# First image of an attention and expert-routing kernel: weights loaded by ScalarE's queue beside x in halves, v of image 1 between two maxima, the row of maxima ahead of k's remainder

## What is computed

```
q = jnp.einsum('mc,bcn->bmn', wq, xf)          # 32 x 1024 for each of 4 images
k = jnp.einsum('mc,bcn->bmn', wk, xf)
v = jnp.einsum('mc,bcn->bmn', wv, xf)
att = jnp.einsum('bmi,bmj->bij', k, q)
att = jax.nn.softmax(att, axis=2)
agg = jnp.einsum('bij,bmj->bmi', att, v)
out = x + jnp.einsum('cm,bmn->bcn', wo, agg).reshape(b, c, h, w)
...
t = t + _L1_attn_ref(_ln_t(t))                 # softmax(t t') t over 1024 tokens
t = t + _L1_ffn_ref(_ln_t(t), ...)             # router, best 2 of 8 experts
```

## Time and profile before

| what | us |
|---|---|
| median of 3 runs | 219.84 (218.81 to 220.49) |
| the profiled execution, its own time | 220.04 |
| its span in the profile | 218.3 |
| TensorE matmul busy in the span | 203.7 |
| VectorE busy | 144.7 |
| ScalarE busy | 107.5 |
| GpSimd busy | 62.1 |

### The profile page before, as it was taken

How to read it: one execution, slowest core, us unless ns; L and a number is a source line. 1 busy time by engine, 2 the same in 40 slices (tenths; PEclk the granted TensorE clock), 3 DMA queues, 4 the chain that set the end, 5 groups by cost and what they waited for, 6 DMA issues and landing times.

```text
span 218.3 us, 2929 instructions
## 1 busy us (share of the span) xinstructions
PE 203.7 (93%) x1073; PEld 104.7 (48%) x1073; DVE 144.7 (66%) x359; ACT 107.5 (49%) x166; POOL 62.1 (28%) x75
## 2 busy tenths in 40 slices
PE   6799998989999899998999999899999999898993
PEld 2463744454634335553443545344344433387773
DVE  2579947978564994566488754727693372898970
ACT  2540676548644646476275536656544666301110
POOL 8222021403000300003003359800359750027250
PEclk9799999999999999999999999999999999999999
DMA  4853000000000000000000000020000002000021
GB/s 107 148 128 67 3 0 0 0 2 3 2 0 0 0 0 3 0 0 0 3 2 0 0 3 2 0 48 0 3 0 0 0 3 50 0 0 3 0 48 48
DMA packets 3341, 3.67 MB, mean 17 GB/s; under 512 B 2176, under 2 KB 2432, under 8 KB 3328
## 3 DMA queue, kind: packets, MB, share of 16 engines
q1 hardware_dynamic: 3328, 3.50, 7.5%
HBM read 2.45 MB, written 1.05 MB: 16 GB/s over the span
## 4 chain that ended last, share of the span: by engine, by line
PE 66%; DVE 22%; ACT 4%; POOL 3%; DMA 2%; issue 2%; SPq 0%; DVEq 0%; POOLq 0%
PE acc L489 21%; DVE rowmax L1108 9%; PE ring L550 6%; PE ring L595 6%; PE ring L551 5%; PE ring L482 5%; PE ring L464 4%; PE acc L625 3%; POOL sm L367 3%; PE ring L442 2%; DMA xin<-in_x 2%; PE ring L526 2%; PE ring L537 2%; PE ring L443 2%; DVE stats L1141 1%
## 5 line engine op out<-in xcount | busy, mean ns | idle before, releaser
L900 ACT ACTIVATE prob<-ring,shift 128x1024 f32<-128x1024 f32 x32 | 35.6, 1112 | 27.6 <-PE ring L551 27.5
L1108 DVE TENSOR_REDUCE rowmax<-ring 128x1 f32<-128x1024 f32 x32 | 38.0, 1218 | 13.4 <-PE ring L464 13.3
L367 POOL TENSOR_TENSOR sm<-sm,minus_half 128x8 f32<-128x8 f32 x8 | 15.8, 1974 | 101.8 <-DVE sm L1151 101.8
L897 ACT ACTIVATE prob<-ring 128x1024 f32<-128x1024 f32 x32 | 31.9, 1023 | 17.8 <-PE ring L482 17.7
L489 PE MATMUL acc<-prob,u 128*64 128x512 f32 x128 | 31.0, 606 | 0.0
L489 PE MATMUL acc<-prob,val 128*64 128x512 f32 x128 | 31.0, 605 | 0.0
L1247 DVE TENSOR_TENSOR prod<-ring,gate 128x1024 f32<-128x1024 f32 x16 | 19.4, 1220 | 9.3 <-PE ring L595 8.8
L550 PE MATMUL ring<-zst 128*128 128x512 f16 x64 | 24.5, 384 | 0.4 <-DVE rowmax L1108 0.4
L551 PE MATMUL ring<-zsw,zst 128*128 128x512 f16 x64 | 24.3, 379 | 0.0
L464 PE MATMUL ring<-qst,kst 96*128 96x512 f32 x64 | 22.6, 437 | 0.5 <-DVE rowmax L1108 0.4
L482 PE MATMUL ring<-kst,qst 98*128 98x512 f32 x64 | 21.3, 425 | 0.8 <-DVE rowmax L1108 0.4
(11 more groups left out here) (156 smaller groups left out, 312.1 us busy)
## 6 DMA issues: line engine op xcount, KB each, us to landing
xin<-in_x SPq DMA_DIRECT2D x8, 256.0 KB, 4.1
out<-ob SPq DMA_DIRECT2D x6, 128.0 KB, 2.3
e_in<-in_L_ffn_expert_w SPq DMA_DIRECT2D x2, 128.0 KB
out<-ob SPq DMA_DIRECT2D x4, 64.0 KB, 2.0
eb_in<-in_L_ffn_expert_b SPq DMA_DIRECT2D x8, 2.0 KB
wo<-in_L_conv_wo SPq DMA_DIRECT2D x2, 8.0 KB, 2.5
r_in<-in_L_ffn_router_w SPq DMA_DIRECT2D x2, 2.0 KB
w<-in_L_conv_wq SPq DMA_DIRECT2D x1, 16.0 KB, 3.5
```

Of the source, the lines that this page charges most:

```text
L367: pool.tensor_tensor(sm[:, 3, :], sm[:, 2, :], minus_half[:, :], ALU.pow).then_inc(s_rs, 1)
L897: act.activation(prob1[:, j % DEEP, :], flat(filled(act, f"st{j}", b)), ACT.Exp).then_inc(s_p1, 1)
L900: act.activation(prob2[:, j % DEEP, :], flat(filled(act, f"s{j}", b)), ACT.Exp, bias=shift[:, :], accum_out=rsum2[b % 2][:, j:j + 1]).then ...
L1108: dve.tensor_reduce(rowmax[:, tile:tile + 1], flat(filled(dve, f"mx{tile}", b)), AX.X, ALU.max).then_inc(s_mx, 1)
```

## The change

Three things change, all in the first 27 us. **Loads:** the three weight transfers are issued by ScalarE's queue, ahead of everything else on ScalarE; SyncE's queue loads x of image 0 in four transfers of 64 x 512, and ScalarE rounds the first half as soon as it is there. `w1` is written by one instruction in place of three, the second half of x is rounded behind the weights, and q's first projection no longer waits for v's weights. **v of image 1** is projected by TensorE between the maxima of tiles 5 and 6 of image 0, in place of after k of image 1; three pairs of filler matmuls go. ScalarE copies it out ahead of q and k of image 1. **The row of maxima** of image 0 is copied by VectorE ahead of k's remainder of image 1.

```diff
--- before.py
+++ after.py
@@ -41,7 +41,8 @@
 
 
 
-HEAD = [("w3", 0), ("q", 0), ("k", 0), ("vx", 0)] + per_tile("mx", 0) + [("q", 1), ("k", 1), ("vx", 1), ("mr", 0)]
+HEAD = [("w3", 0), ("q", 0), ("k", 0), ("vx", 0)] + per_tile("mx", 0)[:6] + [("vx", 1)] + per_tile("mx", 0)[6:] + [
+    ("q", 1), ("k", 1), ("mr", 0)]
 
 FIRST = [("st0", 0), ("st1", 0), ("mx0", 1), ("st2", 0), ("mx1", 1), ("st3", 0), ("mx2", 1), ("mx3", 1), ("st4", 0),
          ("mx4", 1), ("st5", 0), ("mx5", 1), ("st6", 0), ("mx6", 1), ("st7", 0), ("mx7", 1), ("mr", 1), ("po", 0)]
@@ -189,6 +190,7 @@
         s_w3 = sem("w3_loaded")
         s_wol = sem("wo_loaded")
         s_ew = sem("experts_loaded")
+        s_x0 = [sem(f"x0_part_loaded{part}") for part in range(2)]
         s_x = [sem(f"x_loaded{b}") for b in range(B)]
         s_wr1 = sem("weights_rounded")
         s_wts = sem("weights_split")
@@ -298,9 +300,10 @@
                 for h in range(2):
                     sp.dma_start(xin[h * C:(h + 1) * C, b, :], x[b].rearrange("c h w -> c (h w)")).then_inc(s_x[b], 16)
 
-            load_x(0)
-            for n, w in enumerate((wq, wk, wv)):
-                sp.dma_start(w3[n * M:(n + 1) * M, :, :], w.unsqueeze(1).to_broadcast([M, 2, C])).then_inc(s_w3, 16)
+            first = x[0].rearrange("c h w -> c (h w)")
+            for part in range(2):
+                for h in range(2):
+                    sp.dma_start(xin[h * C:(h + 1) * C, 0, chunk(part)], first[:, chunk(part)]).then_inc(s_x0[part], 16)
             sp.wait_ge(s_const, 1)
             for h in range(2):
                 sp.dma_start(wo4[:, 2 * h, :], wo).then_inc(s_wol, 16)
@@ -447,6 +450,8 @@
 
             def project_v(b):
                 buf = take("vx", b)
+                if b:
+                    pe.wait_ge(s_xs, b + 2)
                 for tile in range(T):
                     toks = xst[b % 2][:, col(tile):col(tile) + P]
                     o = (tile % 4) * (M + C)
@@ -631,25 +636,28 @@
                     pe.matmul(bank[:, :], filler[:, 0:P], filler[:, :], start=True, stop=True)
 
             pe.wait_ge(s_filler, 1)
-            keep_clock(9)
+            keep_clock(8)
             buf = take("w3", 0)
             pe.wait_ge(s_const, 2)
             pe.wait_ge(s_w3, 3 * 16)
             pe.transpose(buf[:, 0, 0:ROW], w3[:, :, :].rearrange("p a c -> p (a c)"), ident[0:ROW, 0:ROW]).then_inc(s_fill, 1)
-            keep_clock(2)
-            pe.wait_ge(s_wts, 3)
+            keep_clock(3)
+            pe.wait_ge(s_wts, 2)
             project_qk("q", 0)
             project_qk("k", 0)
+            pe.wait_ge(s_wts, 3)
             project_v(0)
-            for tile in range(T):
+            for tile in range(T - 2):
                 max_scores(0, tile)
-                if tile >= RING - 1:
+                if RING - 1 <= tile < T - 3:
                     keep_clock(2)
+            project_v(1)
+            for tile in range(T - 2, T):
+                max_scores(0, tile)
             pe.wait_ge(s_wol, 2 * 16)
             pe.transpose(acc2[:, 0:C], wo4[:, :, :].rearrange("p a m -> p (a m)"), ident[0:C, 0:C]).then_inc(s_woT, 1)
             project_qk("q", 1)
             project_qk("k", 1)
-            project_v(1)
             max_row(0)
             keep_clock(4)
 
@@ -941,13 +949,18 @@
                 act.activation(ob[b % 2][:, :], buf[:, 0, :], ACT.Copy).then_inc(s_ob, 1)
 
 
-            act.wait_ge(s_x[0], 32)
-            for h in range(2):
+            def round_x0(h):
+                act.wait_ge(s_x0[h], 32)
                 act.activation(xst[0][:, chunk(h)], xin[:, 0, chunk(h)], ACT.Copy).then_inc(s_xr, 1)
+
+            for n, w in enumerate((wq, wk, wv)):
+                act.dma_start(w3[n * M:(n + 1) * M, :, :], w.unsqueeze(1).to_broadcast([M, 2, C])).then_inc(s_w3, 16)
+            round_x0(0)
             buf = filled(act, "w3", 0)
-            for r in range(3):
-                act.activation(w1[:, :, r, :], buf[:, 0, 0:2 * M].rearrange("p (a m) -> p a m", a=2), ACT.Copy).then_inc(s_wr1, 1)
+            act.activation(w1[:, :, :, :], buf[:, 0, 0:2 * M].rearrange("p (a m) -> p a m", a=2).unsqueeze(2)
+                           .to_broadcast([P, 2, 3, M]), ACT.Copy).then_inc(s_wr1, 1)
             act.activation(vx1[:, 0:M], buf[:, 0, 2 * M:3 * M], ACT.Copy).then_inc(s_wr1, 1)
+            round_x0(1)
             for name, dst, s_rounded in (("q", qst[0], s_qr), ("k", kst[0], s_kr)):
                 k, used = PLACE[(name, 0)]
                 for h in range(2):
@@ -959,9 +972,9 @@
             act.wait_ge(s_const, 3)
             values(0)
             round_x(1)
+            values(1)
             round_q(1)
             round_k(1)
-            values(1)
             max_row(0)
 
             for j in range(3):
@@ -1260,13 +1273,12 @@
 
             split_x0(0)
             buf = filled(dve, "w3", 0)
-            dve.wait_ge(s_wr1, 4)
+            dve.wait_ge(s_wr1, 2)
             dve.tensor_tensor(w2[:, :, :, :], buf[:, 0, 0:2 * M].rearrange("p (a m) -> p a m", a=2).unsqueeze(2)
                               .to_broadcast([P, 2, 3, M]), w1[:, :, :, :].bitcast(F32), ALU.subtract).then_inc(s_wts, 1)
+            split_x0(1)
             dve.memset(vx2[:, M:M + C].bitcast(F32), 0.0)
             dve.tensor_tensor(vx2[:, 0:M], buf[:, 0, 2 * M:3 * M], vx1[:, 0:M].bitcast(F32), ALU.subtract).then_inc(s_wts, 1)
-
-            split_x0(1)
             for name, dst, rows, s_rounded, s_split in (("q", qst[0], slice(M, 2 * M), s_qr, s_qs),
                                                         ("k", kst[0], slice(2 * M, 3 * M), s_kr, s_ks)):
                 k, _ = PLACE[(name, 0)]
@@ -1279,8 +1291,8 @@
             dve.wait_ge(s_const, 4)
             negate_max(0)
             split_q(1)
+            max_row(0)
             split_k(1)
-            max_row(0)
 
             dve.wait_ge(s_woT, 1)
             for h in range(2):
```

## The result

| | before | changed |
|---|---|---|
| median, us | 219.93 (218.81 to 220.49, 4 runs) | 217.13 (217.09 to 217.25, 4 runs) |
| profiled execution, us | 220.04 | 217.16 |
| its span, us | 218.3 | 215.4 |

The ratio is 0.9876, 95% interval 0.985 to 0.9902: 2.8 us faster by the medians, against 216.8 forecast with a range of 216.0 to 218.7.

A forecast was written before the change was run, and what follows sets the result against it. TensorE, busy 203.7 of 218.3 us, was taken as the bound, behind a chain of waits at the start. Loads 2.4 plus row stage 0.6 take 3.0 from 220.04: 217.0, median 216.8, range 216.0 to 218.7.

The forecast's parts named there:

- Loads: Kernel start: earlier weights and x bring the first maxima's scores to 10.5 in place of 12.93, 2.4 us gained.
- that sum: Load times at the start, from 218 GB/s and weights landing 2.5 to 2.9 after issue: 2.4 us gained.
- The choice of full clock: Image 0's projections: TensorE busy 2.6 of 3.40 us in 4.3 to 7.7, so the granted clock stays full.
- the two cases: Image 0's projections: full clock, scores at 10.5, gain 2.4; or fallen clock (22%), scores at 11.6, gain 1.3.
- v among the maxima: Image 0's maxima: TensorE's v of image 1 makes VectorE wait for tile 6, 0.35 us lost.
- The slack behind it: Behind the maxima: q of image 1 rounded at 9.85 after the first maximum, VectorE asking at 10.05; fits by 0.2.
- The row stage: Row of maxima to first attention scores: scores 12.15 behind the first maximum in place of 13.0, 0.85 earlier.
- The part that stays: Row stage: of 0.85 us, 0.6 stays after the second scores wait for k's remainder; bounds 0.3 and 0.9.
- ScalarE's readiness: Start, after the table load: ScalarE may not be ready, delaying x's rounding; halfway costs 0.9 us, 217.7; 6%.
- The slower rival: From tile 5 to the row: with fillers gone, half clock on 5.4 us of work adds 5.2, giving 222.0; 5%.

The follow-up runs named there:

- e6: Changed kernel with x of image 0 back in two whole transfers, weights still on ScalarE's queue: 219.36 us, ratio 0.9996 to the kernel before.
- e12: Changed kernel with 4 fillers in place of 8 ahead of the transpose and 1 in place of 3 behind it: 218.2 us, ratio 0.9928.
- e10: Changed kernel with one pair of fillers put back behind tile 5 of the maxima: 217.45 us, ratio 0.9891 to the kernel before.
- e2: Kernel before with only v of image 1 moved among the maxima, three pairs of fillers lost: 220.65 us, ratio 1.0039.
- e11: e4 with one pair of fillers put back behind tile 5 of the maxima: 219.44 us, ratio 0.9974 to the kernel before.
- e1: Changed kernel with v of image 1 and the row's cast put back, so the new loads alone: 217.66 us, ratio 0.9903.
- e4: Kernel before, old loads, with v among the maxima and the row's cast ahead of k's remainder: 219.96 us, ratio 1.0001.
- e5: Changed kernel with the three weight transfers back on SyncE's queue behind x's four: 219.34 us, ratio 0.9997 to the kernel before.
- e7: Kernel before with 11 fillers in place of 9 ahead of the transpose, 3 in place of 2 behind: 219.15 us, ratio 0.998.

## Why the prediction was right

**Loads.** Forecast and found, in us: weights landed 4.7 and 4.7; x's half 0 rounded from 4.4 and from 4.50; the one copy for `w1` 0.35 and 0.33; chunk 0 of q 6.2 and 6.30, chunk 1 6.95 and 7.03; maxima's scores 10.5 and 10.55. The gain is 2.38 against 2.4.

**What stood behind that sum was less sure than it read.** I took the transfers to share 218 GB/s and the weights to land 2.5 to 2.9 after issue from any queue. e6 shows 4.5 in the company of x in whole transfers; only beside halves is it 3.0. The estimate's rows were those of weights issued behind x, not beside it. Their landing before was 6.1 (3.16 and 2.9), not the 6.19 that the prediction has; nothing in the sum hangs on it.

**The clock.** The choice of full clock was right (1.00 in 7.70 to 11.10), and so was about 1 us as the difference of the two cases (1.1 forecast; e12 against the changed kernel 0.9 to 1.1 by the medians, 0.7 in the profiled executions, where the last two of the eight projection matmuls had the full clock again). But in this execution the way there was not the forecast one. The fillers behind the transpose still went at 0.43 each, three from 5.07 to 6.30, so that TensorE was busy 3.38 of the 3.40 us in place of the forecast's 2.6; the clock had not risen near 4.4 as before but just when q began. That the slow fillers cost nothing is luck: q started 0.06 behind VectorE's remainder of the weights (6.24), the same distance as chunk 1 behind its own (6.97 to 7.03). In e10's profiled execution it went as forecast: the clock rose near 4.6, the fillers were through early, TensorE idled 0.50 ahead of q, was busy 2.85 of 3.40, and no fall followed.

**v among the maxima.** VectorE's gap was 0.35, as forecast. e2 shows it uncovered. The slack behind it was thinner than the forecast's 0.2: q was rounded at 21.31, 10.03 behind the first maximum (9.85 forecast), because q started at 7.80 and not 7.65 behind it, after the transpose of `wo`, which the forecast leaves out. VectorE was ready for it at 21.36. That is 0.05 to spare.

**The row stage.** First scores 12.20 behind the first maximum (12.15 forecast), second 13.36 (13.35). The part that stays is 0.53 (2.91 less 2.38) against 0.6, and the same 0.53 in e11's trace.

**The rivals.** ScalarE's readiness: it rounded 1.04 after the table load's end in the changed kernel and 0.93 after it in e1, so it was ready by then. The Trainium skill (ScalarE: Activation LUTs, What ACT_TABLE_LOAD costs) adds a drain of 1380 ns to the load; behind the load, between it and the first activation, it did not stand here, since 0.93 is less. The slower rival's fall happened, but in kernels whose weights came as late as before (e4, and windows at 0.83 and 0.68 in e5's profiled execution).

**From the profiled execution to the median** I took 0.20 off; found is 2.88 between the profiled executions and 2.80 between the medians. So 216.8 is 0.33 too low: 0.16 between the profiled executions (217.0 and 217.16: 0.07 from the row stage, the rest from the head and from rounding), and 0.17 because the changed kernel, with its narrow range, has hardly any such shift (217.16 and 217.13).

## What to carry to other kernels

Two moves that each cost time can gain together, if one clears the engine or the buffer on which the other waits: read the ring's order and the queue's order for both, and test them together before judging either by itself. A second DMA queue brought nothing here by itself, nor did smaller transfers; together they brought most of 2.4 us, since the engine behind them needed both inputs. And where the start of a kernel scatters by a microsecond between executions, look at the distance of its matmuls' starts there, and try a few fillers more (e7 shrank 1.7 us of scatter to 0.5).

## What was not expected of the hardware

- The granted clock in the windows reads 1.00 from the start on, also while fillers go at 0.43 a matmul (1.5 to 6.3 us). It shows changes, and none before the first; the distance between two starts tells the real level.
- The time of the first rise differs between kernels and executions with the same first microseconds: about 4.4 before, about 6.3 and 6.8 in two profiled executions of the changed kernel, about 4.6 in e10's, which is the same kernel up to there.
- In e4's profiled execution a wait (0.40 in its row) and 1.8 us of v's short matmuls, which TensorE's row counts as busy, came right before a fall to half; with 0.45 us of fillers in that wait no run was that long (e11). The changed kernel's profile has the same stretch without a fall. In e2 the fall came behind a wait of 1.47.
- Of eight maxima in a row VectorE's pace (1.14 each) was the same in every kernel here; only waits moved the end.
